# Twelve products of the identity ahead of each of TensorE's last six steps in a four-layer gated transformer

## The reference

```python
x = x + jnp.tanh(g_xattn[0]) * _L0_xattn_ref(_layernorm(x, axis=-1), ctx_1024, ctx_1024, ...)
x = x + jnp.tanh(g_ffn[0]) * _L0_ffn_ref(...)     # 8 experts, each token takes 2, and a shared one
x = x + jnp.tanh(g_xattn[1]) * _L1_xattn_ref(...)
x = x + jnp.tanh(g_ffn[1]) * _L1_ffn_ref(...)     # one ternary 128 x 128 matrix
x = x + jnp.tanh(g_xattn[2]) * _L2_xattn_ref(...)
x = x + jnp.tanh(g_ffn[2]) * _L2_ffn_ref(...)     # four experts of fixed weight, 256 wide
x = x + jnp.tanh(g_xattn[3]) * _L3_xattn_ref(...)
x = x + jnp.tanh(g_ffn[3]) * _L3_ffn_ref(...)     # 8 experts, each token takes the best one, 512 wide
```

## Time and profile before

| | |
|---|---|
| median of 3 runs | 1217.24 us (1215.01 to 1219.12) |
| profiled execution, its own time | 1219.59 us |
| its span, first to last instruction | 1217.8 us |
| mean granted TensorE clock | 0.932 |
| TensorE busy | 1018.1 us (84%) |
| VectorE, ScalarE, GpSimd busy | 786.5, 630.1, 620.2 us |
| the chain that ended last: TensorE, VectorE, issue, GpSimd, ScalarE | 60%, 17%, 10%, 5%, 5% |

### The profile page before, as it was taken

How to read it: one execution, slowest core, us unless ns; L and a number is a source line. 1 busy time by engine, 2 the same in 40 slices (tenths; PEclk the granted TensorE clock), 3 DMA queues, 4 the chain that set the end, 5 groups by cost and what they waited for, 6 DMA issues and landing times.

```text
span 1217.8 us, 25222 instructions
## 1 busy us (share of the span) xinstructions
PE 1018.1 (84%) x8940; PEld 824.2 (68%) x8940; DVE 786.5 (65%) x1680; ACT 630.1 (52%) x1447; POOL 620.2 (51%) x650
## 2 busy tenths in 40 slices
PE   1599999852999899995887889999999999748793
PEld 0477777642667899984566767677777777538793
DVE  2789999735202756783899988745554568826464
ACT  1444444431222566665676687656655657435462
POOL 0154544410777501725886776754455457552763
PEclk9899999955899899998999999999999999868897
DMA  7950000000111123421000000000050000021334
GB/s 237 314 160 2 1 1 1 1 0 0 46 63 57 42 72 88 114 62 38 23 19 10 2 1 2 2 1 1 2 156 1 1 2 1 6 53 48 80 105 128
DMA packets 79735, 59.13 MB, mean 49 GB/s; under 512 B 13668, under 2 KB 72420, under 8 KB 79429
## 3 DMA queue, kind: packets, MB, share of 16 engines
q1 hardware_dynamic: 73028, 44.03, 12.7%
q0 software_dynamic: 6592, 13.58, 3.6%
HBM read 35.76 MB, written 25.07 MB: 50 GB/s over the span
## 4 chain that ended last, share of the span: by engine, by line
PE 60%; DVE 17%; issue 10%; POOL 5%; ACT 5%; SPq 1%; DMA 1%; DVEq 1%; POOLq 0%; ACTq 0%
PE psS L1098 7%; PE psT L1611 5%; PE psO L1109 5%; PE psO L1675 5%; PE psS L1667 5%; PE psO L1626 3%; PE psO L1037 3%; PE psS L1600 3%; PE psS L1029 3%; POOL sorted_z L1343 2%; DVE rden L744 2%; PE psS L1109 2%; DVE x L1886 2%; DVE ring L732 2%; PE psT L610 2%
## 5 line engine op out<-in xcount | busy, mean ns | idle before, releaser
L1966 POOL TENSOR_TENSOR ring<-ring,mx 128x1024 f32<-128x1024 f32 x96 | 182.2, 1905 | 123.5 <-DVE mx L1851 122.8
L1750 ACT ACTIVATE pT<-psT 128x512 f32<-128x512 f32 x192 | 114.5, 596 | 153.2 <-PE psT L1611 153.1
L1148 ACT ACTIVATE pT<-psS,b1copy 128x128 f32<-128x128 f32 x496 | 141.3, 368 | 90.4 <-PE psS L1098 90.4
L1098 PE MATMUL psS<-ring 128*128 128x128 f32 x992 | 136.1, 282 | 14.6 <-DVE ring L1197 8.7
L1611 PE MATMUL psT<-ident,ring 128*128 128x128 f32 x768 | 124.3, 286 | 16.2 <-POOL ring L1966 9.7
L1098 PEld LDWEIGHTS psS<-ring 128*128 128x128 f32 x992 | 124.7, 197 | 16.9 <-DVE ring L1197 6.9
L806 POOL TENSOR_TENSOR ring<-ring,rden 128x1024 f32<-128x1024 f32 x32 | 75.3, 2355 | 116.9 <-DVE rden L746 116.9
L1843 DVE TENSOR_TENSOR ring<-psS,bias 128x1024 f32<-128x1024 f32 x96 | 112.9, 1218 | 33.7 <-PE psS L1600 33.2
L1611 PEld LDWEIGHTS psT<-ident,ring 128*128 128x128 f32 x768 | 87.3, 144 | 56.7 <-issue 33.8
L1281 POOL DMA_INDIRECT xrows<-sorted_y,rows x64 | 62.1, 971 | 101.2 <-DMA sorted_y<-pT 66.3
L1851 DVE TENSOR_REDUCE mx<-ring 128x16 f32<-128x1024 f32 x96 | 112.1, 1209 | 0.0
(11 more groups left out here) (281 smaller groups left out, 2276.5 us busy)
## 6 DMA issues: line engine op xcount, KB each, us to landing
w<-w_dram SPq DMA_DIRECT2D x34, 256.0 KB, 6.0
sorted_x<-late SPq DMA_DIRECT2D x20, 256.0 KB, 3.8
ring<-sorted_x SPq DMA_DIRECT2D x20, 256.0 KB, 3.4
sorted_y<-pT SPq DMA_DIRECT2D x18, 256.0 KB, 2.5
sorted_z<-blank_dram SPq DMA_DIRECT2D x2, 1584.0 KB, 9.8
ring<-sorted_z SPq DMA_DIRECT2D x12, 256.0 KB, 2.9
xrows<-token_y SPq DMA_DIRECT2D x8, 256.0 KB, 3.5
ctxz<-ctxz_dram SPq DMA_DIRECT2D x1, 1056.0 KB, 11.7
```

The source lines that it names most:

```text
L1098: mm = nc.tensor.matmul(psS[:, j % 2, f * P:(f + 1) * P], wcopy[:, j % 4, 0, f, :], xgT[:, s, t * P:(t + 1) * P], start=True, stop=True)
L1148: op = nc.scalar.activation(hs[:, j % 2, f, :], psS[:, j % 2, f * P:(f + 1) * P], func, bias=b1copy[:, j % 4, f:f + 1])
L1750: nc.scalar.activation(pT[:, u % 2, 4 * h:4 * h + 4, :].rearrange("p a q -> p (a q)"), psT[:, :], ACT.Exp).then_inc(s_pT, 1)
L1966: nc.gpsimd.tensor_tensor(rows_, rows_, mx[:, u % 4, 0:NH].rearrange("p h -> p h ()").broadcast_to([P, NH, SK]), ALU.subtract).then_inc(s_ ...
```

## The change

In the stream's loop on TensorE each step from 48 on begins with twelve products of the identity with itself, into the first 128 columns of `psT`. Ahead of the first of them stands a wait for all 192 exponentials (`s_pT`), after which nobody reads `psT` until the experts' part writes it. Nothing reads what the products leave there. There are six such steps, so 72 products, 144 passes.

```diff
@@ -1675,8 +1675,17 @@
                 mm.then_inc(s_full, 1)
 
+            def keep_clock(count):
+
+                for _ in range(count):
+                    nc.tensor.matmul(psT[:, 0:P], ident[:], ident[:], start=True, stop=True)
+
             pe.wait_ge(*FF[0].ye(GROUPS[0]))
             for n in range(FIRST, FINAL):
+                if n == NB:
+                    pe.wait_ge(s_pT, 2 * NU)
+                if n >= NB:
+                    keep_clock(12)
                 if logits_at(n) is not None and not quick(logits_at(n)):
                     logits(logits_at(n))
```

## The result

The changed kernel took 1221.64 us (median of 8 runs, 1217.99 to 1224.26); the kernel before, beside it, 1217.17 us (8 runs, 1215.01 to 1219.67). The ratio is 1.0032, 95% interval 1.0017 to 1.0047: slower by 3.9 us, 2.1 to 5.7.

A forecast was written before the change was run, and what follows sets the result against it. TensorE's late chain, from norm_rows(23) to the second group's scatters, was taken as the bound. Bursts 50 to 53 cost 10.8 us or more, less saved waits and low-clock time: +2.4 on 1217.24, 1219.6 us; range 1214.5 to 1223.5.

The forecast's parts named there:

- The place: Bursts 50 to 53, from norm_rows(22) to transpose_group(1): cost 10.8 us or more, all but 2.4 us taken back.
- The price of a burst: Twelve products, 24 passes on TensorE: 2.7 us at 2.4 GHz, 5.3 us at 1.2 GHz.
- the upper price of 3.5 us: Full-clock burst priced from the first layer's identity products, latency included; would make the sum +4.8 us.
- the 1.9 us by the page of the Trainium skill: Burst priced at about 81 ns per load and matmul; would bring the sum 2.4 us lower, to no change.
- The idle gap: TensorE's 8.70 us idle ahead of norm_rows(22): bursts 48 and 49 fit free, about 4 us remains, the clock most likely falls.
- The rival in which it lives through the gap: Clock stays full ahead of norm_rows(22): +0.5 us, 1217.7 us; chance 0.12.
- the one in which identity products don't bring it back: Bursts 50 to 53 all at low clock: 15 us later, 1232 us; chance 0.10, including a late return.
- The return of the clock: Full clock 5.6 us after TensorE restarts at norm_rows(22), at 1087.0; mean of 3.8, 6.9 and 6.2 us.
- the forecast's own rule: Each microsecond the clock returns earlier or later is worth half of one: +1.5 with 3.8 us, +3.1 with 6.9.
- the fall at 1113 of now: Clock fall after a 2.49 us TensorE stall ending at 1113.30; whether it recurs was put at 1.7 us either way.
- a delay of TensorE between 1089 and 1121 goes to the end of the program in full: Chain from norm_rows(23) through expert tiles and VectorE to GpSimd's second-group scatter: any TensorE delay there counts fully.
- Behind 1102.8 nothing changes but the shift: After transpose_group(1) starts, later work only moves by the +2.4 us, except for the clock fall at 1113.

The follow-up runs named there:

- The third run: 36 identity products ahead of norm_rows(22) and 24 ahead of norm_rows(23), no others, against the kernel before: 1217.78 us, ratio 0.9989.

## Why the prediction was right, and where it wasn't

- **The place.** The bursts from 50 on, on the chain between norm_rows(22) and transpose_group(1). Shown: the late four alone cost +2.0 us, the first two nothing.
- **The price of a burst.** Priced at 2.7 us at full clock from a distance without latency; the chain shows 2.68 and 2.78. Neither the upper price of 3.5 us nor the 1.9 us by the page of the Trainium skill came.
- **The gap and the clock.** The idle gap, forecast at about 4 us, was 3.85 in the profile after, 5.03 in the repeat, and the clock fell in both. The rival in which it lives through the gap is out, and so is the one in which identity products don't bring it back.
- **The return of the clock.** Taken as 5.6 us, measured 5.0 and 5.3. With half a microsecond for each, the forecast's own rule gives +2.1 for 5.0 us; measured +2.03. The lateness of norm_rows(23) was 1.5 us, forecast 1.8.
- **The step that was wrong** is the last of the sum: "the fall at 1113 of now costs some 1.7 us ... That is 1.7 us either way." It costs nothing. Before, the clock fell there; after, it didn't; the distance from transpose_group(1) to (3) is 20.89 us in both. With slow passes TensorE arrives later and waits 0.67 us ahead of up(9) (so in the run with the two covered bursts, where the clock fell as well), with fast ones it waits 2.29; the view names no releaser, but VectorE's copy of that tile's weights ends 0.1 us before up(9) in each. Behind it stands a wrong reading of the chain: "a delay of TensorE between 1089 and 1121 goes to the end of the program in full" holds only up to VectorE's first addition, at 1106.39. From there to the second it is 14.0 us on VectorE in every profile, whatever the clock did. The third run shows it from the other side: it lost 1.6 us on TensorE behind the second wait, and the second group's scatter came no later for it.
- **What was left out.** The forecast has "Behind 1102.8 nothing changes but the shift". The whole time rose by more than the stretch, 2.9 to 3.9 us as the two ratios have it; the interval of the first, 2.1 to 5.7, reaches the 2.4 of the forecast, the repeat's, 1.8 to 3.9, holds it. The profiles show where most of the rest lies: behind transpose_group(6) the clock is back after 5.1, 5.2 and 5.4 us in the three executions with bursts 50 to 53 (the change, its repeat, the late four alone), and after 3.8, 3.8 and 3.0 in the kernel before, with the two covered bursts and with the gaps filled. From there to down(22) that is 5.58 to 5.73 us, against 4.99, 4.98 and 4.56. Why the bursts should delay this return, some 60 us later, is open, and with one profile of each kernel chance isn't ruled out.

So the chance of 0.72 for "within 0.3%" was on the edge: the ratio came out at 1.0032, just past the bound, and the repeat's at 1.0024, inside it. The place and the price were foreseen. The return of the clock was in part luck: 5.6 us was the mean of three between 3.8 and 6.9, and the runs here have others from 3.0 to 9.7.

No version beats both kernels clearly. Filler in the gaps alone, at 0.9989, is the only one below 1 on the first chip with its whole interval, by a tenth of a per cent, and the same filler with other pieces cost some 10 to 14 us on chips where the gap isn't there. Six a step (0.9984 and 0.9985) and the one gap of sixteen (0.9992), all with intervals reaching past 1, did no harm where they were run. Whether six a step wins on the first chip, whether the gaps filled everywhere would win there, and what the stalls called "remote" are, stays open; none of it was tried.

## What to carry to other kernels

Filler on an engine is free only where the wait behind it ends on another engine's time; price each burst against that wait, one by one, since here two of six were free and four were not. A higher clock is worth what the stretch that it runs in is bound by: 3.4 us where TensorE was the bound, nothing where VectorE was, in either direction. So read which engine's wait hands the delay on: here TensorE ran late by 1.6 us in one run and nobody waited for it. A filler sized to a gap in one trace holds only as long as the gap does; small bursts spread over the steps lost less than long ones when the gap was elsewhere.

## What the hardware showed that was not expected

- Transposes alone brought TensorE's clock from 1.2 to 2.4 GHz, between 1148 and 1150, 5 us into an unbroken row of them.
- Stalls of one length don't decide the clock: behind the waits of 2.3 us ahead of up(9) the first passes are fast in the change (1.13 us for eight) and slow with the gaps filled (2.05). Behind waits of 1.60 us ahead of up(0) sixteen take 2.19 us with the gaps filled and 3.76 with the gaps filled everywhere. And with the gaps filled the clock fell at 1070.6 just as unbroken work began.
- The return of the clock after a restart took 5.0 and 5.3 us in the change and 3.0 behind transpose_group(6) with the gaps filled, but in the run with one gap filled TensorE was busy without a break from 1143.49, and the clock was back only at about 1153.2, 9.7 us later.
- The same program takes about 90 us longer on three of the chips than on the first, and its traces there have stalls of up to 32.0 us on ScalarE and VectorE whose releaser they call "remote", on a program of one core. One of them moved the gap that this change is about.
